# Fewer drains on the vector engine in an attention, feed-forward and delta-rule kernel

## The reference

```
x = x + attn_a(layernorm(x))   # qkv product, elu + 1, cumulative sums over tokens, output product
x = x + ffn(layernorm(x))
x = x + attn_b(layernorm(x))   # k, q, v products, 4-tap causal convolution, delta rule in chunks of 64
x = x + ffn(layernorm(x))

# ffn: 1024 -> 4096 -> 1024, activations rounded to 8-bit steps, weights to -1, 0, 1
h = bit_linear(x, w1)
h = depthwise_conv1d(h, conv_w, conv_b)     # 3 taps along the tokens
h = silu(h)
return bit_linear(h, w2)

# attn_b
k = short_conv(x @ Wk.T + bk, conv_k)       # 4 taps along the tokens; the same for q and v
```

## Time and profile before

| what | us |
|---|---|
| median of 3 runs | 22219.57 |
| lowest, highest | 22205.88, 22257.55 |
| the profiled execution's own time | 22199.69 |
| its span (core 2, the slowest) | 22198.0 |
| spans of the other cores | 22115.0 to 22180.9 |
| busy: PE matmul | 8254.5 (37%) |
| busy: DVE | 8117.3 (37%), 23995 instructions |
| busy: ACT | 1285.3 (6%) |
| busy: POOL | 554.6 (2%) |

### The profile page before, as it was taken

How to read it: one execution, slowest core, us unless ns; L and a number is a source line. 1 busy time by engine, 2 the same in 40 slices (tenths; PEclk the granted TensorE clock), 3 DMA queues, 4 the chain that set the end, 5 groups by cost and what they waited for, 6 DMA issues and landing times.

```text
span 22198.0 us, 169160 instructions; the slowest of 8 cores (22115.0 to 22198.0 us)
## 1 busy us (share of the span) xinstructions
PE 8254.5 (37%) x49436; PEld 5906.9 (27%) x49436; DVE 8117.3 (37%) x23995; ACT 1285.3 (6%) x2560; POOL 554.6 (2%) x644
## 2 busy tenths in 40 slices
PE   2104555222211115555555555556455521212112
PEld 1003433111111113334343433334343311111111
DVE  2443333333444423333333333333433334444432
ACT  0111000000000000000000000000000000000001
POOL 0000000000000010000000000000000000000000
PEclk5556777555555555565656565655555555555555
DMA  5122222100000010010101010101000010000001
GB/s 148 54 69 68 69 63 61 33 18 16 16 15 16 16 32 23 1 31 1 31 1 31 1 31 1 31 1 30 2 12 19 4 32 16 16 15 16 15 18 43
DMA packets 706720, 618.74 MB, mean 28 GB/s; under 512 B 43330, under 2 KB 633730, under 8 KB 703394
## 3 DMA queue, kind: packets, MB, share of 16 engines
q1 hardware_dynamic: 585762, 398.16, 6.1%
q0 software_dynamic: 51200, 167.81, 2.6%
q10 hardware_dynamic: 68864, 41.95, 0.7%
HBM read 549.11 MB, written 58.72 MB: 27 GB/s over the span
## 4 chain that ended last, share of the span: by engine, by line
PE 33%; DVE 32%; DMA 14%; issue 11%; ACT 5%; DVEq 3%; ACTq 1%; SPq 0%; POOLq 0%
DMA t2buf<-s_t 9%; PE bank L1292 7%; PE bank L951 4%; PE bank L1312 4%; PE bank L1160 3%; DVE dPows L1299 3%; PE bank L1017 3%; DVEq L147 3%; PE bank L756 2%; DVE dP L1319 2%; DVE hc L1040 2%; DVE hc L1036 2%; DVE hc L1032 2%; DVE fval L1111 1%; DVE dPows L1306 1%
## 5 line engine op out<-in xcount | busy, mean ns | idle before, releaser
L951 PE MATMUL bank<-m2b,t2buf 128*128 128x256 bf16 (+3 forms) x4608 | 965.8, 390 | 3274.0 <-DMA t2buf<-s_t 2399.1
L1292 PE MATMUL bank<-dPows 64*64 64x64 f32 x9216 | 1514.2, 317 | 1244.0 <-DVE dPows L1299 1104.2
L1292 PEld LDWEIGHTS bank<-dPows 64*64 64x64 f32 x9216 | 1148.2, 212 | 1636.2 <-issue 1636.2
L951 PEld LDWEIGHTS bank<-m2b,t2buf 128*128 128x128 bf16 x4608 | 564.5, 139 | 3672.3 <-issue 3503.4
L1299 DVE COPY dPows<-bank 64x128 f32<-64x128 f32 x2304 | 651.9, 283 | 2104.5 <-PE bank L1292 2104.5
L962 DVE TENSOR_TENSOR fval<-bank,fsc 128x256 f32<-128x256 f32 (+3 forms) x144 | 56.9, 395 | 3385.1 <-PE bank L951 3373.5
L1312 PE MATMUL bank<-dP,dPows 64*64 64x64 f32 x5120 | 843.1, 317 | 1000.1 <-DVE dPows L1306 1000.1
L1160 PE MATMUL bank<-lnB,wstrB 128*128 128x256 f32 x4096 | 976.3, 398 | 184.5 <-DVE bv L1498 70.8
L162 POOL DMA_DIRECT2D t2buf<-s_t x576 | 508.5, 883 | 19807.3 <-ACT hbuf L1045 15948.0
L1312 PEld LDWEIGHTS bank<-dP,dPows 64*64 64x64 f32 x5120 | 639.8, 213 | 1203.4 <-issue 1203.4
L1160 PEld LDWEIGHTS bank<-lnB,wstrB 128*128 128x128 f32 x4096 | 799.5, 199 | 363.7 <-issue 250.9
(11 more groups left out here) (319 smaller groups left out, 14309.4 us busy)
## 6 DMA issues: line engine op xcount, KB each, us to landing
t2buf<-s_t POOLq DMA_DIRECT2D x576, 256.0 KB, 3.6
wstrA<-s_qkv SPq DMA_DIRECT2D x192, 512.0 KB, 4.0
wnat<-fw SPq DMA_DIRECT2D x64, 512.0 KB, 3.2
wnat<-fw SPq DMA_DIRECT2D x16, 2048.0 KB, 7.9
wstrA<-s_proj SPq DMA_DIRECT2D x64, 512.0 KB, 4.0
wstrB<-s_k SPq DMA_DIRECT2D x64, 512.0 KB, 4.0
wstrB<-s_q SPq DMA_DIRECT2D x64, 512.0 KB, 4.0
wstrB<-s_v SPq DMA_DIRECT2D x64, 512.0 KB, 4.0
```

The lines of the kernel that those rows point to most:

```text
L951: e.matmul(b[:, 0:ncol], t2buf.ap()[:, m * 128:(m + 1) * 128], m2b.ap()[:, k * 256 + sc:k * 256 + sc + ncol], start=(k == 0), stop=(k == 31)))
L1292: hv = p.top(lambda e, b=b, la=la, lb=lb, h=h: e.matmul(b[0:64, h * 64:h * 64 + 64], pw(la)[:, h * 64:h * 64 + 64], pw(lb)[:, h * 64:h * 6 ...
```

## The change

A new method `Prog.drain` appends a drain by itself. At the places above, operations that do not depend on each other are put in a row with `drain=False`, and one drain stands between such a row and the next that reads its results. For the convolutions and the normalizing that means another order of loops: first one tap for all 8 blocks, then a drain, then the next tap for all 8. What is computed for each element, and in what order the taps are added, is the same. At lines 763 and 1023 only the drains go, all but the last of a strip.

```diff
+    def drain(self, e):
+        self.ops[e].append(lambda eng: eng.drain())
@@ normalizing (attn_a; the same in attn_b with lnB, mbB, sbB)
                 p.op("v", lambda e, c=c, ln=ln, t0=t0: e.tensor_tensor(
-                    ln, xc(c, t0, WA), mbA.ap()[:, :], OP.subtract))
-                p.op("v", lambda e, ln=ln: e.tensor_tensor(ln, ln, sbA.ap()[:, :], OP.mult))
+                    ln, xc(c, t0, WA), mbA.ap()[:, :], OP.subtract), drain=False)
+            p.drain("v")
+            for c in range(NCH):
+                ln = lnA.ap()[:, c * WA:(c + 1) * WA]
+                p.op("v", lambda e, ln=ln: e.tensor_tensor(ln, ln, sbA.ap()[:, :], OP.mult),
+                     drain=False)
@@ qkv results (line 763)
-                                          bias_qkv.ap()[:, m:m + 1], None, OP.add))
+                                          bias_qkv.ap()[:, m:m + 1], None, OP.add),
+                          drain=(m == 23))
@@ first ffn product (line 1023)
-                    h3[:, m, 2:130], b[:, 0:WF], fsc.ap()[:, 256:384], OP.mult))
+                    h3[:, m, 2:130], b[:, 0:WF], fsc.ap()[:, 256:384], OP.mult),
+                    drain=(m == 31))
@@ ffn convolution, one group
-                        fcb.ap()[:, m:m + 1], OP.mult, OP.add))
+                        fcb.ap()[:, m:m + 1], OP.mult, OP.add), drain=False)
+                p.drain("v")
+                for q in range(8):
+                    m = grp * 8 + q
...
-                        hcv[:, q, 0:n], OP.mult, OP.add))
+                        hcv[:, q, 0:n], OP.mult, OP.add), drain=False)
+                p.drain("v")
+                for q in range(8):
+                    m = grp * 8 + q
...
-                        hcv[:, q, 0:n], OP.mult, OP.add))
+                        hcv[:, q, 0:n], OP.mult, OP.add), drain=False)
@@ conv4
-                    dst, r3[:, c, 3:259], cw_t.ap()[:, c * 4 + 3:c * 4 + 4], None, OP.mult))
-                for j, tap in ((2, 2), (1, 1), (0, 0)):
+                    dst, r3[:, c, 3:259], cw_t.ap()[:, c * 4 + 3:c * 4 + 4], None, OP.mult),
+                    drain=False)
+            for j, tap in ((2, 2), (1, 1), (0, 0)):
+                p.drain("v")
+                for c in range(NCH):
+                    dst = dst_ap_fn(c)
...
-                             dst, OP.mult, OP.add))
+                             dst, OP.mult, OP.add), drain=False)
+            p.drain("v")
```

More of the change, by code:

```diff
@@ L1031, in emit_ffn @@
                     m = grp * 8 + q
-                    hvt1 = p.op("v", lambda e, m=m, q=q, n=n, h3=h3, hcv=hcv: e.tensor_scalar(
+                    p.op("v", lambda e, m=m, q=q, n=n, h3=h3, hcv=hcv: e.tensor_scalar(
                         hcv[:, q, 0:n], h3[:, m, 1:1 + n], fcw.ap()[:, m * 3 + 1:m * 3 + 2],
-                        fcb.ap()[:, m:m + 1], OP.mult, OP.add))
+                        fcb.ap()[:, m:m + 1], OP.mult, OP.add), drain=False)
+                p.drain("v")
+                for q in range(8):
+                    m = grp * 8 + q
                     p.op("v", lambda e, m=m, q=q, n=n, h3=h3, hcv=hcv:
@@ L1485, in emit_attn_b @@
                 p.op("v", lambda e, c=c, ln=ln, t0=t0: e.tensor_tensor(
-                    ln, xc(c, t0, WB), mbB.ap()[:, :], OP.subtract))
-                p.op("v", lambda e, ln=ln: e.tensor_tensor(ln, ln, sbB.ap()[:, :], OP.mult))
+                    ln, xc(c, t0, WB), mbB.ap()[:, :], OP.subtract), drain=False)
+            p.drain("v")
+            for c in range(NCH):
+                ln = lnB.ap()[:, c * WB:(c + 1) * WB]
+                p.op("v", lambda e, ln=ln: e.tensor_tensor(ln, ln, sbB.ap()[:, :], OP.mult),
+                     drain=False)
             hv_ln = p.sem["v"].cur()
```

## The result

| | before | after |
|---|---|---|
| median of 10 runs, us | 22222.12 | 21535.42 |
| ratio to before, 95% interval | | 0.9697 (0.9676 to 0.9719) |
| the profiled execution's own time | 22199.69 | 21545.7 |
| weight preparation | 1816.8 | 1801.4 |
| attn_a | 2098.0 | 2078.7 |

The change makes the kernel 3.0% faster (the ratio of the two medians is 0.9691, inside the interval); 21616 was predicted (2.7%), with a range of 21540 to 21900. Taken by the ratio, on the 22219.57 us from which the prediction started, it is 21546, 6 us inside. The stages are cut at the first instruction of each in the trace, and each number is the median of the 8 cores.

What follows compares the result with a forecast made beforehand. The kernel was taken as a serial chain where vector engine savings count in full. Ffn convolution 451.6, conv4 112.9 and normalizing 38.8 sum to 603 us, giving 21596 profiled and a median of 21616, range 21540 to 21900.

Steps and rivals of the forecast that it cites:

- the margin that was added below: Range's low end set at 21540, under the forecast's own 21560, for a slightly better overlap of vector operations.
- The serial chain: Whole kernel: engines mostly work in turn; nothing lies beside the vector engine in the convolution, so its savings count in full.
- Which boundaries count: Ffn convolution 2688 (451.6 us), conv4 672 (112.9), normalizing 231 (38.8); drains at lines 763 and 1023 give nothing.
- The thin cover of the first ffn product: Line 1023: evacuations still wait 0.17 and 0.40 us for PE, so 992 drains give nothing; uncovered, up to 92 us.
- The price of one boundary: Between vector operations: removing a drain saves the 93 ns gap plus 75 ns of early start, 168 ns.
- The gap of 93: Idle time the drain leaves ahead of the convolution's line 1040, 93 ns each, given back without the drain.
- the early start: Without a drain, the next vector operation begins 75 ns before the one ahead has ended.
- Instruction supply: Idle "issue" time, 0.2 to 11.9 us a line before, could eat as much as 18 us of the gain.
- Gap alone: Rival, 10%: operations with pointer scalars in a row don't overlap, so only 93 ns a boundary goes; 334 us, median 21886.
- Hidden load: Rival, 7%: the 60 ns pointer scalar load is also hidden behind the operation ahead; 805 us, median 21415.
- The pipe that empties anyway: Rival, 4%: each vector operation still waits for the one ahead with its full gap; no change, 22220.
- Held operations: Rival "Slower", 4%: undrained convolution operations wait for the one ahead, then load their scalar; 67 ns lost each, median 22446.

Runs made afterwards that it cites:

- the 64-partition kernel: The changed kernel with the ffn convolution and its silu on 64 of the 128 partitions, the other half left out; one run of 21559.47 us.
- the constants: The changed kernel with plain constants in place of the pointer scalars (factor and bias) in the ffn convolution; one run of 21372.67 us.

## Why the prediction was right, and by how much it was off

The saving was forecast as 603 us and came out as 673 by the ratio and 687 by the medians, 12 to 14% more. The forecast's own range, 21560 to 21670, was missed. That the result touches the stated range at all is owed to the margin that was added below, down to 21540, and not to a term of the sum.

*The serial chain.* Right. What the silu no longer waited, 505.6 us, is what the two ffn stages lost, 504.6. Nothing lay beside the convolution. Where 7.2 us of waiting a group were forecast, the trace shows 6.91.

*Which boundaries count.* Right: 3591 of them, 10387 drains left, and the 1176 drains of the evacuations worth nothing (0.9997). The thin cover of the first ffn product held. One reason given for it is not what the rows show: the pause of PE in the earlier trace rows ends with "issue" and not with the vector engine's semaphore. In the whole trace before, PE waited at that line for the evacuations 4.8 us in 22 places, and 0.2 us in one after the change.

*The price of one boundary, 168 ns.* This is the term that was mis-sized. It is 182 ns for the multiply-adds (0.445 to 0.263, 0.578 to 0.396), 182 for the normalizing (0.517 to 0.335), and 182 to 186 where a TENSOR_SCALAR is one of the two (0.439 to 0.257 behind one, 0.449 to 0.263 ahead of one), 183 in the mean. The gap of 93 was right; the early start is 352 - 263 = 89 ns and not 75. I subtracted the 75, read where operations had 64 partitions and stood in a row, from the duration of one with 128 partitions that stood behind a drain. The full number of partitions adds 9 ns to a duration and nothing to the distance between starts (the 64-partition kernel). A place behind a drain adds 5 ns to a duration (352 against 347) and some 6 to the distance: in the changed kernel the first multiply-add of a row starts its follower after 0.269 us, the others after 0.262 to 0.263, and with the own semaphore in the drain's place the first does so after 0.263 too. So the early start that I should have taken off the 352 is 75 + 9 + 5 = 89. The right way was open in the rows of before: the distance of starts in the earlier trace rows is 0.20, and 128 elements more lengthen a multiply-add by 484 - 352 = 132 ns (after the change 0.396 - 0.263 = 0.133 between starts), which leaves some 67 ns fixed; with a pointer scalar 60 more. That gives 0.260 for the multiply-adds, where 0.263 was measured, and 0.333 for the normalizing, where 0.335 was. With it the price would have been 0.445 - 0.260 = 185 ns. The Trainium skill, "Vector Engine (DVE) Microarchitecture Reference", section 5.2, has this form with about 75 ns fixed; here 0.202 - 0.133 = 69 ns were measured, without pointer scalars.

*Instruction supply.* The prediction feared that it could eat 18 us. Instead "issue" at the three lines fell from 14.4 us to 0.4, with nearly half of the instructions gone from there. It stayed at 14.4 where the order changed and the drains didn't, so it goes with the drains; that it is the supply of instructions is my reading, and no row shows it.

With these, 3591 x 0.183 + 14 = 671 us, and the stages without the weight preparation lost 648 in the median (19 + 252 + 124 + 253). Attn_b's 124 is below the 145 that its 791 boundaries should give. Two more traces have the same attn_b: it takes 9324.1 us with constants and 9329.1 with 64 partitions in the ffn convolution, 138 and 133 less than before. So a part of the gap is the spread between executions; what is left, some 7 to 12 us there, stays open.

*The rivals.* Gap alone (21886): refuted by starts of 0.263. Hidden load (21415): refuted by the constants, 61 ns in a row. The pipe that empties anyway, which the Trainium skill gives as a rule ("VectorE: DVE Perf Modes", section "The DRAIN you can't avoid"): refuted; with 128 partitions the next operation starts 84 ns before the end of the one ahead (347 - 263), with 64 partitions 75 (338 - 263). The same section of the Trainium skill adds that a next operation that isn't held starts earlier, and with this sentence the trace agrees. Held operations (22446): refuted.

## What to carry to other kernels

Read the cost of a short vector operation from the distance of starts in a row, not from its duration: here a multiply-add of 0.352 us costs 0.445 with a drain behind it and 0.263 without. Order independent operations in a row and fence the row once, or wait on the engine's own semaphore for what was made 8 places back, where the engine works alone on the path; where it waits for another engine anyway, drains can be free, as the 1176 of the evacuations were here.

## What the runs showed of the hardware that was not expected

Each pointer scalar of the ffn convolution costs 60 to 61 ns of the vector engine's pace, and two in one operation cost 121. The TENSOR_SCALAR of 128 elements with constants starts every 0.136 us, 66 ns sooner than the multiply-add with a constant (0.202): as if it moved through 128 elements in half the time. Line 1187 of the changed kernel bears that out: with 256 elements and one pointer scalar it starts every 0.263 us, which is 0.136, 60 ns for the scalar and 67 ns for 128 elements more, where the multiply-add takes 133 ns for them. What the engine does differently there no run shows. A wait of the engine on its own semaphore, met 8 operations before, cost nothing measurable (0.256 to 0.263 with it, 0.257 to 0.263 without).
